# Normalisations cut into steps, and the first two batches normalised alone, in a fused attention and spiking-FFN kernel

## What is computed

```python
def _mlstm_cell(q, k, v, igate_w, igate_b, fgate_w, fgate_b, ln_scale):
    ifg = jnp.concatenate([q, k, v], axis=-1)
    ig = (ifg @ igate_w.T + igate_b).T
    fg = (ifg @ fgate_w.T + fgate_b).T
    log_f = jax.nn.log_sigmoid(fg)
    cs = jnp.cumsum(log_f, axis=1)
    log_D = where(tril, cs[:, :, None] - cs[:, None, :], -inf) + ig[:, None, :]
    max_log_D = jnp.max(log_D, axis=-1, keepdims=True)
    D_mat = jnp.exp(log_D - max_log_D)
    C = einsum('hsd,htd->hst', qh, kh) / np.sqrt(DH) * D_mat
    normalizer = jnp.maximum(jnp.abs(C.sum(-1, keepdims=True)), jnp.exp(-max_log_D))
    h = jnp.einsum('hst,htd->hsd', C / (normalizer + EPS), vh)   # heads side by side
    return layernorm(h) * ln_scale

def _L0_ffn_ref(x, W_fc, W_proj):
    h = jnp.square(relu(x @ W_fc.T))
    y = h @ W_proj.T
    # 5 steps: mem = 0.9*mem + y - (mem > 1);  spikes = mem > 1
    return sum(spikes) / 5

x = x + tanh(g_xattn[0]) * mlstm(layernorm(x), ctx, ctx)
x = x + tanh(g_ffn[0]) * ffn(layernorm(x))
```

## Time and profile before

| | |
|---|---|
| median of 3 runs | 617.12 us (615.51 to 617.72) |
| profiled execution: span | 615.3 us |
| PE busy | 571.4 us, 93% |
| DVE busy | 526.3 us, 86% |
| ACT busy | 485.8 us, 79% |
| POOL busy | 493.3 us, 80% |
| mean granted TensorE clock | 0.980 |

### The profile page before, as it was taken

The page is one execution under the profiler, slowest core; times in us unless marked ns, Lnnn a source line. Parts: engine busy times, 40 slices in busy tenths (PEclk is TensorE's granted clock), DMA queues, the critical chain, the costliest instruction groups (busy, mean ns, idle before and its releaser), DMA issues.

```text
span 615.3 us, 17747 instructions
## 1 busy us (share of the span) xinstructions
PE 571.4 (93%) x6032; PEld 479.2 (78%) x6032; DVE 526.3 (86%) x1291; ACT 485.8 (79%) x1011; POOL 493.3 (80%) x541
## 2 busy tenths in 40 slices
PE   0568988999999999999999999999999999999995
PEld 0357888887888888888788888888888888887894
DVE  4789889989989898989989898989999888878446
ACT  3776878897888888888888788888888777776673
POOL 4878889996997889887997889887997887955542
PEclk9995989999999999999999999999999999999998
DMA  8775736664664637662663637752675427401002
GB/s 271 168 145 115 160 74 124 168 139 95 124 149 96 155 84 127 171 146 70 123 163 83 158 83 131 187 126 70 121 167 130 87 48 148 121 4 35 0 2 70
DMA packets 73193, 71.34 MB, mean 116 GB/s; under 512 B 8720, under 2 KB 68752, under 8 KB 73104
## 3 DMA queue, kind: packets, MB, share of 16 engines
q1 hardware_dynamic: 71888, 70.00, 50.5%
q10 hardware_dynamic: 1216, 0.21, 0.2%
HBM read 27.44 MB, written 8.39 MB: 58 GB/s over the span
## 4 chain that ended last, share of the span: by engine, by line
PE 82%; SPq 7%; DMA 3%; ACT 2%; issue 2%; DVE 2%; POOL 1%; ACTq 0%; POOLq 0%; DVEq 0%
PE z_ps L1069 28%; PE y_ps L1135 26%; PE qk_ps L773 4%; PE arg_ps L758 4%; PE misc_ps L503 4%; SPq L706 3%; PE misc_ps L569 2%; SPq L553 2%; PE pv_ps L822 2%; PE pv_ps L820 2%; PE pv_ps L821 2%; PE pv_ps L897 2%; DMA x<-w_proj_t 2%; PE y_ps L1164 1%; PE arg_ps L1135 1%
## 5 line engine op out<-in xcount | busy, mean ns | idle before, releaser
L802 POOL TENSOR_TENSOR c_lo<-decay 128x512 bf16<-128x512 f32 x128 | 132.7, 1043 | 31.9 <-DVE decay L792 31.8
L1112 POOL TENSOR_TENSOR sq_lo<-w_raw,sq_hi 128x512 fp32r<-128x512 f32 (+1 forms) x96 | 111.8, 1166 | 39.6 <-ACT w_raw L1092 39.3
L1069 PE MATMUL z_ps<-x_hi,wfc_hi 128*128 128x512 f32 (+1 forms) x288 | 114.4, 397 | 1.8 <-ACT w_raw L1079 1.8
L1069 PE MATMUL z_ps<-x_hi,wfc_lo 128*128 128x512 f32 (+1 forms) x288 | 106.1, 368 | 0.0
L1069 PE MATMUL z_ps<-x_lo,wfc_hi 128*128 128x512 f32 (+1 forms) x288 | 105.9, 368 | 0.0
L1135 PE MATMUL y_ps<-sq_hi,wpr_hi 128*128 128x512 f32 (+1 forms) x256 | 103.8, 406 | 0.0
L1135 PE MATMUL y_ps<-sq_hi,wpr_lo 128*128 128x512 f32 (+1 forms) x256 | 97.4, 380 | 0.0
L1135 PE MATMUL y_ps<-sq_lo,wpr_hi 128*128 128x512 f32 (+1 forms) x256 | 97.1, 379 | 0.0
L792 DVE TENSOR_TENSOR decay<-qk_ps,decay 128x512 f32<-128x512 f32 x128 | 87.0, 680 | 9.4 <-ACT decay L784 6.5
L784 ACT ACTIVATE decay<-arg_ps,lqk_col 128x512 f32<-128x512 f32 x128 | 86.6, 677 | 10.5 <-PE arg_ps L761 9.5
L1153 DVE SCALAR_TENSOR_TENSOR spikes<-y_ps,spikes 128x1024 bf16<-128x1024 f32 (+1 forms) x64 | 73.8, 1153 | 1.2
(11 more groups left out here) (193 smaller groups left out, 1727.8 us busy)
## 6 DMA issues: line engine op xcount, KB each, us to landing
x_in<-x SPq DMA_DIRECT2D x32, 256.0 KB, 3.2
kT_in<-ctx_cols SPq DMA_DIRECT2D x32, 256.0 KB, 3.2
v_in<-ctx_rows SPq DMA_DIRECT2D x32, 256.0 KB, 4.3
k_stack<-kT_hi SPq DMA_DIRECT2D x64, 128.0 KB, 3.2
k_stack<-kT_lo SPq DMA_DIRECT2D x64, 128.0 KB, 3.7
q_stack<-qT_hi SPq DMA_DIRECT2D x64, 128.0 KB, 4.1
q_stack<-qT_lo SPq DMA_DIRECT2D x64, 128.0 KB, 4.3
out<-w_raw SPq DMA_DIRECT2D x32, 256.0 KB, 3.4
```

Of the source, the lines that this page charges most:

```text
L802: e.tensor_tensor(c_lo[i % NCH][:, :], c, top(c), ALU.subtract).then_inc(sem("c_lo"), 1)
L1069: ins = e.matmul(z_ps[:, tokens(q)], lhsT, rhs, start=(n == 0), stop=(n == len(terms) - 1))
L1112: e.tensor_tensor(sq_lo[n % NSQ][:, tokens(q)], relu[n % NRE][:, tokens(q)], sq_hi[n % NSQ][:, tokens(q)].bitcast(fp32), ALU.subtract).the ...
```

## The change

Five things change together.

- **LN1 of the first two batches.** The groups of LN1 become (batch 0), (batch 1), then pairs. Batches 0 and 1 have no offset and no application on ACT; a new DVE step `ln1_first` subtracts the mean and multiplies, in two operations of 128x256 each.
- **Normalisations as steps.** Statistics, their aggregation, logarithm, exponential, scaling and so on are steps of their own (`ln1_bn`, `ln1_stats`, `ln1_log`, `ln1_rstd`, `ln2_bn`, ..., `x1_scale`, `x1_step`), with their own semaphores in the place of `link`, and other steps can stand between them. `square` is cut the same way.
- **The row sum's bound.** Of `h_norm`'s seven DVE operations, the three at L915 to L917 become one ACT operation (absolute value of the row sum, 128x16, in PSUM) and one DVE operation, `(denom + EPS) max floor`. POOL adds EPS to the floor once per group (`floor_eps`).
- **gate_w** comes from the host in the layout that the buffer wants (128 runs of 384 B in the place of 768 runs of 64 B).
- **New orders** in all five lists. Among them: `setup_tanh` behind the first two LN1 groups on ACT; `setup_rows` ahead of the first statistics on DVE, the fixed rows first on POOL; k of batch 0 loaded ahead of x on SP, x of batches 2 and 3 ahead of the FFN's weights, k of batch 3 and the second weight behind the `a_rows` of batch 0; at the end, `count_T` of job 16 ahead of the last y step of job 17 on PE, and `out_step` of job 16 ahead of the spikes of job 17 on DVE.

```diff
+    LN1 = [(0, 1), (1, 1)] + [(b, 2) for b in range(2, B, 2)]
+    FIRST = 2
...
-            for dst, src in ((gw_raw[:, :, :], gate_w.rearrange("(c p) g -> p c g", p=P)), (gate_bias[:, :], gate_b)):
+            for dst, src in ((gw_raw[:, :, :], gate_w), (gate_bias[:, :], gate_b)):
...
-        def rstd_of(e, rstd, lnv, mv):
-
-            link(e, "scalar", e.activation(lnv[:, :], mv[:, :, 1], ACT.Ln, bias=eps_col[:, :]))
-            return e.activation(rstd[:, :], lnv[:, :], ACT.Exp, scale=-0.5)
...
+        def ln1_log(e, i):
+            if not 0 <= i < len(LN1):
+                return
+            e.wait_ge(sem("ln1_stats"), ln1_end(i))
+            if i == 0:
+                e.wait_ge(sem("cols_ready"), 1)
+            if i - 1 >= 0:
+                e.wait_ge(sem("ln1_rstd"), i)
+            n = LN1[i][1] * ST
+            e.activation(lnv1[:, 0:n], mv1[i % 2][:, 0:n, 1], ACT.Ln, bias=eps_col[:, :]).then_inc(sem("ln1_log"), 1)
...
+        def ln1_first(e, b):
+
+            e.wait_ge(sem("ln1_rstd"), b + 1)
+            for t in range(ST):
+                dst, src = xln_views(b, t)
+                ins = e.tensor_scalar(dst, src, mv1[b % 2][:, t, 0:1], rstd1[b % 2][:, t:t + 1], ALU.subtract, ALU.mult)
+            ins.then_inc(sem("xln_first"), 1)
...
-            link(e, "vector", e.scalar_tensor_tensor(most[:, :, :], row_sum, -1.0, least, ALU.mult, ALU.max))
-            link(e, "vector", e.tensor_tensor(denom, row_sum, most[:, :, :], ALU.max))
-            link(e, "vector", e.tensor_scalar(denom, denom, EPS, None, ALU.add))
...
+            e.activation(denom, pv_heads[:, :, :, DH], ACT.Abs).then_inc(sem("h_abs"), 1)
...
+            e.wait_ge(sem("h_abs"), b + 1)
+            if b == GROUPS[g][0]:
+                e.wait_ge(sem("floor_eps"), g + 1)
+            e.scalar_tensor_tensor(denom, denom, EPS, floor[g % 3][:, 0:ST, row:row + NH],
+                                   ALU.add, ALU.max).then_inc(sem("h_denom"), 1)
```

More of the change, by code:

```diff
@@ L154, in build_block @@
         x1 = [sb(f"x1_{i}", [P, 2 * ST, D], fp32) for i in range(NX1)]
-        stat3 = sb("stat3", [P, ST, 6], fp32)
+        stat3 = [sb(f"stat3_{i}", [P, ST, 6], fp32) for i in range(2)]
         mv3 = [sb(f"mv3_{i}", [P, ST, 2], fp32) for i in range(2)]
@@ L1830, in vector_program @@
+            x1_scale(e, 5)
             cmul(e, 6, 2)
[L1831 to L1832 removed]
             x1_step(e, 5)
+            ln3_bn(e, 5)
             ln3_stats(e, 5)
@@ new lines, in vector_program @@
+            x2_lo_step(e, 6)
+            cmul(e, 8, 0)
+            h_scale(e, 7)
+            h_add(e, 7)
+            h_denom(e, 7)
+            h_recip(e, 7)
+            h_norm(e, 7)
+            cmul(e, 8, 1)
+            ln2_bn(e, 7)
+            ln2_stats(e, 7)
+            q_lo(e, 12)
+            x1_scale(e, 7)
+            cmul(e, 8, 2)
+            x1_step(e, 7)
+            cmul(e, 8, 3)
+            state_own(e, 8)
+            ln3_bn(e, 7)
+            cmul(e, 9, 0)
+            ln3_stats(e, 7)
```

3523 lines of the change are left out of this document (2702 added, 821 removed), and 13 rows, old and new, of the table SLOTS.

## The result

The changed kernel takes 630.25 us (median of 4 runs, 629.0 to 633.16) against 616.32 us for the kernel before on the same chip: ratio 1.0214, 95% interval 1.0182 to 1.0247. It is 2.1% slower, and outside the range. The profiled execution has a span of 627.2 us, 11.9 more than before.

The account below looks back on a forecast made before the run. PE was taken as the bound from 104 to 600 us, DVE as nearest to full in the ramp. Start +0.8, row sum -1.1, moved loads 0, middle 0 and end +1.0 gave 617.1 + 0.7 = 617.8 us, range 612.0 to 622.5.

Parts of the forecast that it names:

- first transpose: Start, PE: begins at about 15.0 us instead of 15.95, with the second load still late.
- first decay argument: Start, PE: at 34.0 us instead of 33.25, +0.8, taken between 0 and +1.5; five table loads on ACT.
- late load: Start: DVE idle 2.83 us for batch 1's load, until 9.29; the forecast kept this lateness with whatever is loaded second.
- row sum and split steps, ramp: Ramp, batches 4 to 6: two small DVE operations fewer per batch gain 1.1 us; bounds -2.5 and +1.0.
- moved loads: k of batch 3 loaded later, so POOL's split of it comes up to 2 us later; taken as 0, up to +1.0.
- steady stretch, 104 to 600 us: Middle: PE is full, so the DVE saving is worth 0 and the extra ACT and POOL operations are hidden.
- rival 4: Middle: waiting for ACT's absolute value, or a new order, costs PE 0.1 us per batch, +3.2, 621.0 us; chance 0.08.
- end: End: job 17's last y step waits behind job 16's transposes, so its spikes begin later, +1.0 (+0.5 to +1.3).
- first rival: Start: the late second load came with gate_w's 768 small runs and is gone, -2.0 there, 615.0 us; chance 0.16.
- third rival: Start, ACT: table switches cost more than their rows, 5.1 us over four loads, 622.5 us; chance 0.14.
- second rival: Start and ramp: work taken from DVE and an earlier start come through in full, -5.6, 611.5 us; chance 0.20.
- The signs: Wrong if PE's first decay argument came before 31 or after 37 us, or PE waited over 3 us in the middle.

Follow-up runs that it names:

- before_scan_repeated: The kernel before, with the cumulative maximum of DVE's group arithmetic done four times over from the fifth group on; 649.90 us, ratio 1.0541.
- denom_on_dve: The changed kernel with the row sum's bound on DVE as before, three operations, no absolute value on ACT, no EPS on POOL; 630.05 us, ratio 1.0211.
- tanh_first: The changed kernel with tanh and its table load at the head of ACT's list, as before, two table loads instead of five; 627.28 us, ratio 1.0166.
- steps_in_old_order: The changed kernel's steps in the lists of before on all engines, tanh first, row sum's bound on DVE with three operations; 616.39 us, ratio 0.9989.
- before_first_two_alone: The kernel before with gate_w's new layout, batches 0 and 1 normalised alone and tanh first, all other orders kept; 615.33 us, ratio 0.9955.

## Why the prediction was wrong: the steps one by one

The walk, in the prediction's order:

| step | predicted | measured |
|---|---|---|
| first transpose | 15.0 (load late), about 2.8 earlier if not | 12.31 |
| first decay argument | +0.8, or -2.0 without the late load | -2.1 |
| row sum and split steps, ramp | -1.1 (-2.5 to +1.0) | with the term above -1.4 at the first z of job 2, in this pair of traces |
| moved loads | 0 (up to +1.0) | no delay: see below |
| steady stretch, 104 to 600 us | 0; rival 4: +3.2 | +12.3 |
| end | +1.0 (+0.5 to +1.3) | +1.07 |

-1.4 + 12.3 + 1.1 = +12.0, and the spans differ by 11.9. The medians differ by 13.9; single times of the changed kernel lie up to 4 us apart, so the 2 us between the two are not a term of the sum. The -1.4 is the least certain of the three: it is taken against the one late start of before.

**The steady stretch: the step that failed.** The prediction read the earlier trace rows as "PE full, so a saving is worth 0, and a loss needs a wait that starves PE", which held. It then dismissed the loss with DVE's 63 us of slack, and that is where it failed. The slack is an average. Once per group DVE does six operations on 32 partitions, and the next `x_lo` and `x` for PE stand right behind them; there a delay has no slack to use up. before_scan_repeated shows it: three short operations more per group, and PE is idle for 21.4 us more (33 us slower in all, with the clock). The fourth rival had the right stretch, and named the new orders beside a wrong wait (ACT's absolute value: denom_on_dve, no difference), but it had a price four times too small and a chance of 0.08.

The second half of the failure is in how the order was read. The prediction compared each engine's list with its own list of before. No list shows which rows of two engines meet in time, and the 12 us come from a meeting: the new POOL list has 4 us of work at the place where the old one had nothing for 2.4 us. That those 2.4 us of idle POOL were worth something could have been read from the trace of before: in one group, at 209.81, the input of the maxima `am` (L655) took 0.66 us while POOL's `kw_lo` ran, and in the group before, at 140.70 with POOL idle, 0.41.

A page of the Trainium skill speaks of this, and was not drawn on. "SBUF — State Buffer", section "Who interferes with whom", has DVE and GpSimd share one pair of ports to SBUF as an exclusive lock: a DVE operation with two inputs in SBUF, or one in a two-port mode, and a POOL operation that reads SBUF don't run together, and the loser is blocked entirely rather than slowed. The trace agrees: the two-input row maximum takes 0.41 to 1.34 us, the one-input 32x128 operation 0.27 to 1.20, and a row maximum of 1.33 us ends at 217.75, 0.28 us behind the POOL operation that had begun before it. Whether the one-input operation runs in a two-port mode no view here tells. With that rule the question "what does POOL do while DVE has its group arithmetic" would have been asked before the run.

**The start.** The first rival's term, -2.0 with a chance of 0.16, is what this pair of traces gives, -2.1, but that is luck. Its reason, the 768 small runs of gate_w, isn't borne out: with the same 768 runs batch 1 was in time in three other traces (6.14 to 6.44). The prediction took a wait of 2.83 us for a load, seen in one execution, for a property of the kernel. Against those three traces the first decay argument (30.8 to 32.3 in the eight traces with the start of the changed kernel, 29.38 to 32.87 in theirs) and the first z of job 2 (112.5 to 114.3, and 111.8 to 114.1) are not clearly earlier, so that the new start gains anything with its five loads isn't shown. ACT's first load starts at 8.28 and `q_hi` at 15.97, where 10.9 and 18.6 were predicted.

**The table loads.** Five, as predicted, and the third rival falls. ACT after:

```profile
9.57 0.29 ACT L462 ACTIVATE lnv<-mv,eps_col 128x2 f32<-128x2 f32 x1
9.88 1.28 ACT L473 ACT_TABLE_LOAD   x1
11.18 0.20 ACT L473 ACTIVATE rstd<-lnv 128x2 f32<-128x2 f32 x1
11.46 1.28 ACT L462 ACT_TABLE_LOAD   x1
```

A load takes 1.28 us and has at most 0.08 us on either side, also with work waiting behind it. The drain of about 1380 ns that the Trainium skill gives ("ScalarE: Activation LUTs", section "What ACT_TABLE_LOAD costs") isn't there in this trace; the row decided rightly against it. What the loads cost is small: tanh_first does without three of them, has `q_hi` at 11.29, 4.7 us earlier, and its span is 1.8 us shorter.

**The row sum.** -1.1 was taken for the ramp, 0 for the middle. denom_on_dve (630.05 against 630.25) shows a saving too small to measure; the bounds hold it. Of the -5.6 that the second rival hoped for in all, start and ramp show -1.4 in this pair of traces, which is within what starts of one kernel differ by.

**The moved loads and the end.** Nothing came of the later k: the first product with v starts at 40.3 us after, at 40.9 before. The end cost 1.07 us for 1.0, by the mechanism given.

**The range.** 612.0 to 622.5 was built from the bounds of start, ramp and end, some 3 us to a side. No case in it held a loss in the stretch that makes up 80% of the span, save one at 0.1 us per batch. When a change rewrites the orders of all engines there, the bound of that term isn't 0 but what a stall per batch or group can cost: before_scan_repeated gives 3.6 us of waiting per group for 2.1 us of delay, and 2.7 more by the clock, and that scale belonged into the range.

**The signs.** The prediction was to be wrong if the first decay argument came before 31 or after 37, or if PE had waits of over 3 us in the middle. The first came at 31.20 and PE's longest wait there is 2.01 us, so neither sign spoke. What did was the sum that it expected unchanged, PE's busy time from 104 to 600 us: 486.65 in the place of 494.95. A loss made of many short holes needs a sum as its sign, not a longest wait.

**What stays open.** 4.4 us of the middle, after the clash and the end are taken off, and how the clash divides between DVE's waiting and POOL's. tanh_first's gain shrinks from 4.6 us at the first decay argument to 2.1 at the first z of job 2, and no run says why. That the cut steps themselves cost 0 to 1.7 us in the stretch (steps_in_old_order) lies within what two traces of one kernel can differ by. Why the second load was late in the profiled execution of before is open too.

## What to carry to other kernels

Ask of a new order not only what moved on each list but what two engines that share something now do at the same time, above all at the places where the bound engine waits for the very next instruction; an engine's idle time there can be what keeps another one fast. Average slack says nothing of such a place: lengthen the suspected operations, or shorten them, and see whether the span follows. A wait for a load that one trace shows should be looked for in a second trace before it becomes a term. Of this change the parts without the orders (gate_w's layout, batches 0 and 1 alone, tanh first) were together the better kernel: before_first_two_alone, 615.33 us, ratio 0.9955 (0.9934 to 0.9976).
